# Moving work of a Mamba scan from VectorE and TensorE to GpSimd, and moving the part ahead of the scan beside another layer

## The reference

```
h[t] = exp(delta[t] * A[d,n]) * h[t-1] + (delta[t] * x[t]) * B[t,n]
y[t] = sum over n of h[t] * C[t,n]     (+ D * x[t], then times silu(z))
```

## Time and profile before

| | us |
|---|---|
| median of three runs | 5841.52 |
| the profiled execution's own time | 5854.07 |
| its span, first to last instruction | 5852.3 |

### The profile page before, as it was taken

The page is one execution under the profiler, slowest core; times in us unless marked ns, Lnnn a source line. Parts: engine busy times, 40 slices in busy tenths (PEclk is TensorE's granted clock), DMA queues, the critical chain, the costliest instruction groups (busy, mean ns, idle before and its releaser), DMA issues. The chain is left out here.

```text
span 5852.3 us, 66174 instructions
## 1 busy us (share of the span) xinstructions
PE 4549.0 (78%) x20516; PEld 2163.4 (37%) x20516; DVE 3845.6 (66%) x8884; ACT 2735.1 (47%) x5086; POOL 1114.1 (19%) x1324
## 2 busy tenths in 40 slices
PE   5687786977779776787777878788786877879777
PEld 2243243432444224442244422444234432344334
DVE  5867855679455885558855587556875568556554
ACT  2364452645436444364443544435454454426443
POOL 2412310033110420104201042010420114101100
PEclk8898887988889888898888987888887988889678
DMA  3211210112101110012100121001210012101000
GB/s 122 79 46 44 64 45 3 51 47 63 37 3 51 63 53 31 16 44 65 58 19 22 41 65 54 19 28 38 67 53 15 34 40 67 55 5 51 1 26 6
DMA packets 113278, 247.72 MB, mean 42 GB/s; under 512 B 12096, under 2 KB 20800, under 8 KB 112880
## 3 DMA queue, kind: packets, MB, share of 16 engines
q1 hardware_dynamic: 112896, 243.17, 13.2%
HBM read 240.44 MB, written 2.69 MB: 42 GB/s over the span
## 5 line engine op out<-in xcount | busy, mean ns | idle before, releaser
L714 POOL TENSOR_TENSOR heads_work<-heads_work,heads_c_all 128x512 f32<-128x512 f32 x384 | 493.4, 1285 | 801.4 <-DVE heads_work L747 801.1
L1426 ACT ACTIVATE heads_prob<-BANKS 128x512 f32<-128x512 f32 (+3 forms) x768 | 384.4, 517 | 313.3 <-PE BANKS L1323 309.1
L691 PE MATMUL BANKS<-heads_work,WF 128*128 128x512 f32 x768 | 485.3, 717 | 28.7 <-POOL heads_work L714 25.1
L738 DVE TENSOR_TENSOR BANKS<-BANKS,m_du 128x512 f32<-128x512 f32 x512 | 357.5, 698 | 175.0 <-PE BANKS L683 173.6
L205 POOL TENSOR_TENSOR rstd<-rstd,WF 128x4 f32<-128x4 f32 x24 | 24.1, 1006 | 1666.7 <-DVE rstd L223 1524.4
L1323 PE MATMUL BANKS<-heads_parts_kT,heads_parts_qT 64*128 64x512 bf16 (+3 forms) x768 | 246.9, 365 | 70.8 <-DVE heads_nmax L1450 35.6
L2065 DVE CUSTOM_DVE_ANT_0 attn_biased<-BANKS,attn_toep 128x512 f32<-128x512 f32 x384 | 262.2, 684 | 43.9 <-PE BANKS L1963 39.7
L683 PE MATMUL BANKS<-m_bcs,WB 96*128 96x512 bf16 x512 | 217.8, 428 | 87.7 <-DVE heads_work L747 51.3
L2044 ACT COPY attn_probt<-BANKS 128x512 f32<-128x512 f32 x384 | 223.5, 582 | 126.6 <-PE BANKS L1970 124.1
L2036 ACT ACTIVATE attn_prob<-attn_biased,attn_nmax 128x512 f32<-128x512 f32 x384 | 280.3, 730 | 1.1 <-DVE attn_nmax L2065 1.0
L1450 DVE CUSTOM_DVE_ANT_0 BANKS<-BANKS,WF 128x384 f32<-128x384 f32 (+3 forms) x512 | 243.5, 499 | 53.7 <-PE BANKS L1323 51.6
(11 more groups left out here) (916 smaller groups left out, 10478.6 us busy)
## 6 DMA issues: line engine op xcount, KB each, us to landing
heads_c_all<-c_rows SPq DMA_DIRECT2D x384, 256.0 KB, 3.1
attn_toep<-bias_line SPq DMA_DIRECT2D x96, 448.0 KB, 4.4
last_x_w<-in_w SPq DMA_DIRECT2D x48, 512.0 KB, 3.5
s_c_all<-c_rows SPq DMA_DIRECT2D x64, 256.0 KB, 3.2
yheads_c_all<-c_rows SPq DMA_DIRECT2D x64, 256.0 KB, 3.2
yattn_toep<-bias_line SPq DMA_DIRECT2D x16, 448.0 KB, 4.3
zattn_toep<-bias_line SPq DMA_DIRECT2D x16, 448.0 KB, 4.3
ylast_x_w<-in_w SPq DMA_DIRECT2D x8, 512.0 KB, 3.9
```

The lines of the kernel that those rows point to most:

```text
L691: nc.tensor.matmul(SUM, ident, work[:, m % RW, :], start=(n == 0), stop=(n == NS - 1)).then_inc(acc, 1)
L714: nc.gpsimd.tensor_tensor(work[:, m % RW, :], work[:, m % RW, :], c_all[:, m % RC, :], ALU.mult).then_inc(rd, 1)
L738: V.tensor_tensor(DRIVE[s % 2], DRIVE[s % 2], du[:, d, t, :], ALU.mult).then_inc(drv, 1)
L1426: nc.scalar.activation(prob[:, i % PR, lo:hi], bank("T", i)[:, lo:hi], ACT.Exp).then_inc(exped, 1)
```

## The change

**In the scan.** Even and odd steps differ now.

- The rows of B go to DRAM with those of C (`bc_dram` in place of `c_dram`). For odd steps SyncE spreads the B row with a DMA (32 more for each scan), and GpSimd makes the product B * du into the `work` tile (`drive`). TensorE's spreading matmul and VectorE's product stay for even steps alone, in one PSUM bank.
- GpSimd, after the product with C of an odd step, adds the odd tile to the even one before it. TensorE sums only that (32 matmuls for each scan in place of 64).
- The decay of odd steps goes into PSUM bank 2 (which DRIVE has freed); that of even steps goes into two SBUF tiles. So each scan has one input in PSUM and one in SBUF, as before.
- Two more steps of look-ahead for the C rows (four buffers in place of three), and other waits to match.

**Around it.** The part ahead of the scan gets `delay=70.0`: in `last`, its due times run from 67 to 123, beside the end of the experts, the norms and the memory layer. A few due times of it, of the memory layer and of the gate's move in the expert layers are shifted.

```diff
 def mamba_scan:
-        decay = [own[:, i, :] for i in range(RD - 2)] + [XNM..., XTM[:, :]]
+        b_all, c_all = st.sb("b_all", [P, RB, SEQ]), st.sb("c_all", [P, RC, SEQ])      # RB 3, RC 4
+        SUM, DRIVE, OUT = PS[0], PS[1], PS[1]
+        def decay(m):
+            return PS[2] if m % 2 else (XNM..., XTM[:, :])[m // 2 % 2]
...
         def sync(sp):
+            yield at(-6)
+            sp.dma_start(b_all[:, 0, :], row(0, 1)).then_inc(b_ld[0], 16)
             for m in range(STEPS):
-                yield at(m - 3)
+                yield at(m - 5)
+                if m % 2 and m + 2 < STEPS:
+                    k = m // 2 + 1
+                    if k >= RB:
+                        sp.wait_ge(drv[1], k - RB + 1)
+                    sp.dma_start(b_all[:, k % RB, :], row(0, m + 2)).then_inc(b_ld[k % RB], 16)
...
         def tensor(pe):
-                if s < STEPS:
+                if s < STEPS and s % 2 == 0:
...
-                m = s - LATE
-                if m >= 0:
+                m = s - LATE - 1
+                if m >= 0 and m % 2 == 0:
-                    pe.wait_ge(rd, m + 1)
+                    pe.wait_ge(paired, m // 2 + 1)
...
         def scalar(act):
-                yield at(m - 2) + 0.3 * STEP
-                if m >= RD:
+                yield at(m - 1) + 0.2 * STEP
+                held = 2 if m % 2 else 4
+                if m >= held:
...
         def gpsimd(pool):
+            def drive(s):
+                pool.wait_ge(b_ld[k % RB], 16 * (k // RB + 1))
+                if s >= RW:
+                    pool.wait_ge(paired, (s - RW) // 2 + 1)
+                nc.gpsimd.tensor_tensor(work[:, s % RW, :], b_all[:, k % RB, :], du[:, d, t, :], ALU.mult).then_inc(drv[1], 1)
             for m in range(STEPS):
+                if m == 0:
+                    yield at(0)
+                    drive(1)
+                if m % 2 and m + 2 < STEPS:
+                    yield at(m) + 0.2 * STEP
+                    drive(m + 2)
                 yield at(m) + 0.9 * STEP
                 (work *= C, as before)
+                if m % 2:
+                    pool.wait_ge(rd, m + 1)
+                    even = work[:, (m - 1) % RW, :]
+                    nc.gpsimd.tensor_tensor(even, even, work[:, m % RW, :], ALU.add).then_inc(paired, 1)
...
         def vector(dve):
+                if s % 2 == 0:
+                    dve.wait_ge(b_cast, s // 2 + 1)
+                    V.tensor_tensor(DRIVE, DRIVE, du[:, d, t, :], ALU.mult).then_inc(drv[0], 1)
...
-                V.tensor_tensor_scan(work[:, s % RW, :], decay[s % RD], DRIVE[s % 2], 0.0,
+                V.tensor_tensor_scan(work[:, s % RW, :], decay(s), work[:, s % RW, :] if s % 2 else DRIVE, 0.0,
 the stage "last":
-            streams = [mamba_pre(st, lambda: one(xs, b + 2))] if pre_next else []
+            streams = [mamba_pre(st, lambda: one(xs, b + 2), delay=70.0)] if pre_next else []
```

More of the change, by code:

```diff
@@ L106, in bass_mk_seq @@
     ident_b = WBF("ident_b")
-    c_dram = nc.dram_tensor("c_rows", [2, NS, SEQ], F32, kind="Internal").ap()
+    bc_dram = nc.dram_tensor("bc_rows", [2, 2 * NS, SEQ], F32, kind="Internal").ap()
     bias_dram = nc.dram_tensor("bias_line", [H, 1024], F32, kind="Internal").ap()
@@ L634, in vector, with delayed, late @@
                 V.tensor_tensor(delta[:, d, :, :], delta[:, d, :, :], soft[:, d, :, :], ALU.add).then_inc(dd, 1)
+        def delayed(program):
+            def late(engine):
+                for t in program(engine):
+                    yield t + delay
+            return late
         pieces = Pieces()
         pieces.engines = ("sync",)
-        pieces.sync, pieces.tensor, pieces.scalar, pieces.gpsimd, pieces.vector = sync, tensor, scalar, gpsimd, vector
+        pieces.sync, pieces.tensor, pieces.scalar, pieces.gpsimd, pieces.vector = map(
+            delayed, (sync, tensor, scalar, gpsimd, vector))
         return pieces
@@ L648, in mamba_scan @@
         work = st.sb("work", [P, RW, SEQ])
[L649 to L652, removed]
+        b_all, c_all = st.sb("b_all", [P, RB, SEQ]), st.sb("c_all", [P, RC, SEQ])
+        SUM, DRIVE, OUT = PS[0], PS[1], PS[1]
+        b_cast, dec, scn, rd, paired, acc = (st.sem(n) for n in ("b_cast", "dec", "scn", "multiplied", "paired", "acc"))
+        drv = st.sem("drv_even"), st.sem("drv_odd")
         yev, emptied, ych, outp = (st.sem(n) for n in ("yev", "emptied", "ych", "outp"))
-        c_ld = [st.sem(f"c_ld{i}") for i in range(RC)]
-        SUM, DRIVE, OUT = PS[0], (PS[1], PS[2]), PS[1]
+        b_ld, c_ld = ([st.sem(f"{n}_ld{i}") for i in range(k)] for n, k in (("b", RB), ("c", RC)))
+        def decay(m):
+            return PS[2] if m % 2 else (XNM[:, :, :].rearrange("p j d -> p (j d)"), XTM[:, :])[m // 2 % 2]
         def step(i):
@@ L682, in tensor @@
                     row = WBF("pick", 96)[:, n:n + 1]
[L683 to L685 removed]
+                    nc.tensor.matmul(DRIVE, bc(row, [96, P]), bcs[:, d, :], start=True, stop=True).then_inc(b_cast, 1)
+                m = s - LATE - 1
+                if m >= 0 and m % 2 == 0:
                     n = m % NS
                     yield at(s) + 0.45 * STEP
[L688 removed]
+                    pe.wait_ge(paired, m // 2 + 1)
                     if n == 0 and m:
                         pe.wait_ge(emptied, m // NS)
[L691 removed]
+                    nc.tensor.matmul(SUM, ident, work[:, m % RW, :], start=(n == 0), stop=(n == NS - 2)).then_inc(acc, 1)
             yield TAIL + STEP * LATE + 4.0
@@ L860, in scalar @@
                 yield at + 0.2 + step * i + 1.0
-                if i == TURN + 1:
-                    gate.move(act, UP[slot["turn", 0] % 2])
                 if not both:
@@ L872, in scalar @@
                     nc.scalar.activation(s1[:, i % 2, :], UP[slot["up", i] % 2], ACT.Silu, bias=b_up[:, i:i + 1]).then_inc(acted, 1)
+                if i == TURN:
+                    yield at + 0.2 + step * (i + 0.5) + 0.4
+                    gate.move(act, UP[slot["turn", 0] % 2])
         def vector(dve):
@@ L993, in tensor @@
             total(NG - 1)
+            yield G0 + STEP * NG + 1.4
             pe.wait_ge(yev, 1)
```

48 lines of the change are left out of this document (24 added, 24 removed).

## The result

The changed kernel takes 6021.93 us (median of 4 runs, 6020.33 to 6028.94), the kernel before beside it 5843.96: a ratio of 1.030, with a 95% interval of 1.027 to 1.033. I had forecast 5800. It is slower by 178 us, outside my range of 5705 to 5885.

What follows compares the result with a forecast made beforehand. VectorE, 84% busy beside attention, was taken as the nearest but not only bound. Scan beside attention -63, moved part -30, scan alone +51 give -42 us: 5812 from the profiled 5854.07, 5800 as a median; range 5705 to 5885.

Steps and rivals of the forecast that it cites:

- `s0`, +51 (45 to 65): Scan alone, once: GpSimd becomes the bound at 5.3 us a pair of steps, 51 us longer, bounds 45 to 65.
- -22.5 + 7: Scan beside attention, per stage: 32 products off VectorE save 22.5 us; rope-part instructions stretched by GpSimd cost 7 (0 to 14).
- 15 by my count: Rope parts under the skill's exclusive port lock: 15 us a stage in place of 7, total 56 us worse; not adopted.
- Removed from TensorE: ... 59 us: Scan beside attention, per stage: 32 spreads of 0.42 and 64 passes of 0.71 leave TensorE, 59 us.
- Where TensorE bounds, the gain is TensorE's: Scan beside attention, 750 to 770: TensorE has 1.8 us less a pair; the same 0.7 a pair taken as gain.
- Rival 4: Attention stages: with less work TensorE's clock falls, 9.6 us longer a stage, 5866 in all; chance 0.10.
- rival 1: Beside attention, causal T tiles and first layer's tail: GpSimd's queue bounds, 2 us longer a stage, 5876; chance 0.20.
- 6.3 us as lost: Causal layer's T tiles: GpSimd's selects cover 9 pairs, whose saving of 0.70 us each is taken as lost.
- a tenth of a microsecond: Scan beside attention: cost of the pair add's wait for the product GpSimd has just issued.
- the sum's six microseconds of slack: Scan beside attention: TensorE's sum is due some 6 us after the odd scan, for 2.6 us of work; no cost expected.
- The moved part, -30: Part ahead of the scan, moved beside the memory layer, six times: 5 us less an iteration, 30 in all.
- rival 3: Moved part in `last` gains nothing, 5829; sign: memory takes over 92 us; chance 0.12.

Runs made afterwards that it cites:

- e4: Kernel e1 without the pair adds: GpSimd still makes the odd products, TensorE sums all 64 tiles; 5788.71 us, ratio 0.988, and 0.991 when run again.
- e1: The changed kernel's new scan with the last stage of the kernel before, old due times included; 5986.71 us, ratio 1.023.
- e5: The kernel before with the odd tiles' summing matmuls taken away, so TensorE sums only the 32 even tiles; 5918.47 us, ratio 1.010.
- e14: Kernel e1 with zero-weight matmuls at the odd tiles' turns in TensorE's queue, no new wait; 5939.54 us, ratio 1.012.
- e13: Kernel e5 with TensorE's wait for GpSimd's product put back at each odd tile's turn, but no matmul; 5909.37 us, ratio 1.008.
- e6: The kernel before with only the pair adds on GpSimd, TensorE summing 32 tiles, VectorE still making all drives; 5976.80 us, ratio 1.020.

## Why the prediction was wrong, step by step

**`s0`, +51 (45 to 65): right in mechanism, 42 measured.** GpSimd is busy 153.5 of 166 us, back to back:

```profile
202.35 1.26 POOL L750 TENSOR_TENSOR s_work<-s_work,s_c_all 128x512 f32<-128x512 f32 x1
...
203.57 1.26 POOL L738 TENSOR_TENSOR s_work<-s_b_all,m_du 128x512 f32<-128x512 f32 x1
...
204.80 1.26 POOL L750 TENSOR_TENSOR s_work<-s_work,s_c_all 128x512 f32<-128x512 f32 x1
...
206.14 1.26 POOL L754 TENSOR_TENSOR s_work<-s_work 128x512 f32<-128x512 f32 x1
...
207.36 1.26 POOL L750 TENSOR_TENSOR s_work<-s_work,s_c_all 128x512 f32<-128x512 f32 x1
```

A pair takes 207.36 - 202.35 = 5.0 us. I had 5.3: 0.2 for waits of its own that do not show.

**The products and the port: right in size, half right in place.** I forecast -22.5 + 7 from products and rope. In e4, the products alone, the lines add up to -22.4 + 7.2. But I had the 7 in the rope parts, and these and the norms took 2.9 of it; 3.8 are in the conversions and small subtractions of the maxima's parts, which take 371 ns in e4, before 187:

```profile
L1499 DVE TENSOR_TENSOR heads_nmax<-heads_nmax,heads_parts_q 128x16 f32<-128x16 f32 x16 | 5.9, 371 | 0.6
```

The rule of the Trainium skill that I had cited (SBUF — State Buffer, "Who interferes with whom"), the loser blocked for a whole instruction, gave 15 by my count for the rope parts; the measured 7.2, for the products alone, is the size of my row's 7 and half of the 15. With the adds on top (e1) VectorE is 6.1 us busier than in e4, which I had not counted. The long scans (1212 to 1216 ns) stayed as they were.

**"Removed from TensorE: ... 59 us": this is the step that failed.** I set that work down as free or as a gain ("Where TensorE bounds, the gain is TensorE's"). (Its size is a little high too: 64 passes of 0.71 count overlap twice, by busy time half the sum is 40 and the whole 53.5.) Half the sum gone costs 7.8 us a stage by itself (e5), at a clock of 0.74 in place of 0.85, and of e1's 14.8 us over the kernel before 8.1 go back when zeros are multiplied in its place (e14). For the spreads the step held: in e4, where they alone are gone from TensorE, the clock stays at 0.84 and the stage gains. Rival 4 named this, with 9.6 us a stage, its sign (clock below 0.8, measured 0.70). By the Trainium skill (TensorE: Matmul & The Clock Gate, "The HAM clock gate") activity releases the throttle; e14 agrees: more matmuls, clock from 0.71 to 0.82 in the mean. I gave the rival 0.10 on one argument, "at clocks of 0.86 and 0.83, both last 285.1 to 285.2", and that was no measurement. Between real borders the kernel before's seven stages last 279.4 to 282.3 at 0.86 and 0.87, and 290.3 to 291.8 at 0.82 and 0.83. My own trace held the sign that I denied: the slow-clocked stages are 8 to 12 us longer. Which of the two leads, it does not tell; that took e5 and e14.

**The GpSimd queue: rival 1, half right.** I took 6.3 us as lost and priced the rival at 2 us longer a stage. The waits I named are there (TensorE for the adds 11.5 us, weighings for selects 3.9), and the tail of the causal layer is GpSimd's. But its price hangs on TensorE's speed: e14, equally full, loses little in that layer (137.8, before 135.7). In the second layer, where I had left GpSimd out, the adds' cost stays at any clock (e1 153.5, e14 154.1, with a quarter of each add 149.4, without them 145.3; before 149.6). Of the 8.2 us between e4 and e1 there, VectorE's busy time takes 4.6 (118.7 to 123.3).

**The add that "a tenth of a microsecond" should cost, and the sum's six microseconds of slack:** TensorE waited for the adds, 11.5 us in the first stage, so that slack was used up at times. What this costs is not shown apart; e13 says only that the odd tiles' waits don't matter in the old scan.

**The moved part, -30: wrong sign, +21 to +28.** I gave the memory layer 87 us, it takes 97.0 (rival 3's sign, over 92). VectorE is busy 72.2 of them, as I had worked out (73.5). The idle rest is 25, not 16. The experts' 73.3 was right (73.9). I bounded that idle time well (77 to 113) and then chose low in it. What VectorE waits for in that stretch:

```profile
DVE last_heb L1124 <- ACT last_vrc L1069: 7.3, 4, 4.3
DVE XO L1139 <- PE BANKS L1039: 4.1, 1, 4.1
DVE last_red L1135 <- PE BANKS L1031: 4.0, 1, 4.0
DVE last_mu L1091 <- ACT last_qkv L1046: 3.7, 1, 3.7
```

In all four an instruction of the memory layer itself waits for ScalarE or TensorE, 19.1 us together. In the kernel before, with nothing beside it, VectorE was idle 19.5 us in that layer. So the part ahead, put there, filled almost nothing of that time; no run tests whether another order would.

**In all:** forecast -63 - 30 + 51; measured +109 + 21 + 42. In `heads` rivals 1 and 4 together, not one of them, are what happened, and I had priced neither for the case of both. Their shares do not add up: against e4 the adds cost 22.8 us a stage, of which the filler returns 8.1, a quarter of each add 9.5, no selects 6.7. Without the adds `heads` came out at -56 (7 x -8.0), near my -63; as my sum took the adds as 6.3 us lost in the T tiles and free elsewhere, that nearness is partly luck.

## What to carry to other kernels

Work taken off TensorE is not free: look up the granted clock in each stage that loses matmuls, compare the same stage at two clocks between real events (never between window ends you chose), take the work away alone in a run of its own, and price the remaining matmuls at the lower one. When a change moves work in two ways, ask of each way alone whether it helps: here the product moved to GpSimd gained 8 us a stage, and the add moved with it lost 23. A filler says nothing about a clock until it stands off the critical chain.

## What the runs showed of the hardware that I had not expected

- Useless matmuls can make a kernel faster. Kernel e1 took 1.023 of before's time and with 28 zero-weight matmuls a scan 1.012; TensorE's busy time hardly changed (210.9 us a stage in the mean, then 212.7).
- The granted clock falls inside stretches where TensorE is nearly always busy: 0.53 with 18.2 of 20 us. Waiting for it to be idle is no way to find this.
- Two equal loads on GpSimd (41 us of products in e4, or of adds in e6, a stage) stretched VectorE's instructions by 7.2 and 7.1 us, summed by line. About half of it is in instructions with two SBUF inputs: a 128x16 subtraction went from 187 ns to 372 and to 326, with both loads to 448. The rest is in conversions and scalings with one input.
